# A grouped attention-pooling and per-sample product kernel: first group on raw fp32 operands, two-pass scores, work moved from VectorE to ScalarE and GpSimd

## The chip, the core and the metric

The kernel runs on one core of a Trainium2 chip. The core has TensorE for matrix products (PE in the trace; its weight loads are PEld), VectorE (DVE), ScalarE (ACT), GpSimd (POOL) and SyncE (SP), which issues most DMA. The engines share no clock and meet at semaphores. The metric is the device time of one execution in microseconds (us).

## What is computed

```
attn_in = tanh(einsum('bsd,da->bsa', hidden, W1) + b1)
scores = einsum('bsa,a->bs', attn_in, v)
masked_scores = where(mask, scores[:, None, :], NEG_INF)   # mask by type: prefix, postfix, all but self
p = softmax(masked_scores, axis=-1)
cnt = sum(mask, axis=-1)
pooled = einsum('bjl,bld->bjd', p, hidden) / cnt[..., None]
x = x + pooled
out = x + einsum('bsd,bdh->bsh', x, W[cat_ids]) + b[cat_ids][:, None, :]
```

x is 64 samples of 128 rows by 512 columns, W holds 64 matrices of 512x512, W1 is 512x128, all float32. With M = I + p/cnt (applied to rows) and Wi = W + I, the kernel computes for each sample k: z = x Wi, and out = z + (p/cnt) z + b, since both steps are linear in x.

## The kernel before

There are 16 groups (g) of G = 4 samples (k = 4g + b). x comes transposed, one 1 MB load per group (x_raw, two buffers); the matrix of each sample is one 1 MB load (w_raw, five buffers). Products are held to float32 quality by splitting each operand in a high part in the type fp32r (ScalarE copy, `w_hi`, `xT_hi`) and the rest (VectorE subtraction, `w_lo`, `xT_lo`), and adding three products: hi*hi, lo*hi, hi*lo. D = 512 is cut in DC = 4 chunks of 128, so x*Wi of one sample (`xw`, lines 498 to 511) is 12 matmuls of 128x512.

For each sample: VectorE adds the identity to the diagonal blocks of w_raw (`add_identity`, line 339, 128x512 elements); ScalarE makes w_hi (L255); VectorE makes w_lo (L363); TensorE does xw(k) into PSUM bank ps_y; ScalarE copies it to z_hi (L283), VectorE makes z_lo (L391); TensorE adds p z and the bias in four matmuls (`pz`, L519 to L522); ScalarE copies the sum to out_sb (L289) and SP stores it.

For each group: TensorE does x W1 (`hidden`, L474, 12 matmuls), ScalarE tanh (L261), TensorE the scores (`scores_group`: one matmul of v broadcast with attn, both plain float32, L482, and four small bf16 matmuls that add the mask, L484), VectorE the row maximum (L368), ScalarE four exp with row sums (L268), VectorE 1/(sum*count) and the scaling of the rows (L373, L376, L380), TensorE four transposes (L495), ScalarE and VectorE split the result (mix_hi L276, mix_lo L386).

Each engine's order is written by hand as a loop over k. An engine runs its list in order; a wait holds all that stands behind it. On TensorE a step is xw(k), pz(k-2), and then, by b: the transposes of group g (b = 0), hidden(g+1) (b = 1), scores(g+1) (b = 2), nothing (b = 3). VectorE makes w_lo two samples ahead, ScalarE w_hi three ahead. SP's list: store(k-3), the next x, and the matrix of sample k+7, which waits until w_lo(k+2) has freed its buffer. At the start 40 matmuls on zeros (`warm_up`) run while the first loads are under way; x of group 0 and W of sample 0 come in halves and are split half by half.

Of the kernel before, what the change touches and what calls it, by code (L numbers as in the profile page):

```python
# [25 lines left out]
def program(nc, xg, types, cats, w1, b1, v, w, bias, out):  # L27
# [9 lines left out]
    NX, NW, NH, NL, NZ, NO, NY = 2, 5, 4, 3, 3, 4, 5  # L37

    ctx = ExitStack()
    with ctx:  # L40
# [113 lines left out]
        @block.sync
        def _(sp):
            def load_w(k):
                cat = sp.value_load(cat_row[0:1, k:k + 1], min_val=0, max_val=C - 1)
# [24 lines left out]
            sp.dma_start(v_col[:], v.rearrange("(p a) -> p a", a=1)).then_inc(v_in, 16)  # L182
            sp.dma_start(b1_col[:], b1.rearrange("(p a) -> p a", a=1)).then_inc(b1_in, 16)
# [2 lines left out]
            load_w(2)
# [3 lines left out]
            for t in range(-2, B + 3):  # L190
# [48 lines left out]

# [351 lines left out]
```

## Time and profile before

| | |
|---|---|
| median of 3 runs | 335.98 us (335.58 to 336.35) |
| profiled execution | 336.02 us, span from first to last instruction 334.2 us |
| mean granted TensorE clock | 0.98 |
| PE busy | 317.1 us, 95% |
| DVE busy | 293.0 us, 88% |
| ACT busy | 257.0 us, 77% |
| POOL busy | 4.7 us, 1% |
| DMA | 101.56 MB, mean 304 GB/s |

The profiled execution lies on the median; 1.8 us of it are outside the span. Busy shares are averages over the start and the steady part of the kernel, which have different limits, and must be read stage by stage. Matmul records of TensorE overlap (one lasts 0.39 us, the next starts 0.23 us after it), so the time that one costs is read from the distance of starts.

### The profile page before, as it was taken

The page shows a single profiled execution, that of the slowest core. Times are in us where ns is not written, and L with a number is a line of the kernel's source. Part 1 is how long each engine was busy: PE and PEld are TensorE (multiplying, and loading weights), DVE is VectorE, ACT ScalarE, POOL GpSimd, SP SyncE. Part 2 cuts the span into 40 slices and gives each one's busy share as a digit, 9 for nine tenths or more (in the row PEclk, how much of TensorE's full clock was granted, in tenths as well). Part 3 has the DMA queues.
Part 4 walks back from the last instruction along what each step waited for, and adds up shares of the span by engine and source line. Part 5 has one row for each costly group of instructions (what it writes and reads, how often), then busy time and mean ns, then how long its engine had stood idle before and what let it go on. Part 6 is the DMA issues. An engine that isn't in the chain of part 4 may idle for free.

```text
span 334.2 us, 4766 instructions
## 1 busy us (share of the span) xinstructions
PE 317.1 (95%) x1416; PEld 251.7 (75%) x1416; DVE 293.0 (88%) x305; ACT 257.0 (77%) x373; POOL 4.7 (1%) x19
## 2 busy tenths in 40 slices
PE   7475899999999999999999999999999999999996
PEld 5253678787887878787887878787887878788784
DVE  1559969898998989898998989899998989899860
ACT  2468378796978879696978879697887879697843
POOL 5000000000000000000000000000000000000000
PEclk9969699999999999999999999999999999999999
DMA  6999777998989799898989899898979899784113
GB/s 151 349 424 421 271 297 267 363 328 251 402 289 420 234 373 345 281 381 259 416 267 387 299 370 349 305 351 272 393 261 394 296 335 375 279 273 176 63 63 126
DMA packets 21642, 101.56 MB, mean 304 GB/s; under 512 B 2706, under 2 KB 2706, under 8 KB 11634
## 3 DMA queue, kind: packets, MB, share of 16 engines
q1 hardware_dynamic: 21458, 100.94, 82.5%
q0 software_dynamic: 160, 0.33, 1.0%
q8 instruction: 12, 0.20, 0.2%
q14 instruction: 12, 0.10, 0.1%
HBM read 84.48 MB, written 16.78 MB: 303 GB/s over the span
## 4 chain that ended last, share of the span: by engine, by line
PE 89%; DMA 4%; DVE 3%; SPq 2%; issue 1%; ACT 0%; DVEq 0%
PE ps_y L507 17%; PE ps_y L509 17%; PE ps_y L508 17%; PE ps_pre L474 13%; PE ps_y L522 4%; PE ps_y L520 4%; PE ps_y L519 4%; PE ps_y L521 4%; DMA w_raw<-in_L_cond_W 4%; PE ps_scores L482 4%; PE ps_pT L495 2%; DVE w_lo L363 1%; PE ps_scores L484 1%; DVE xT_lo L350 1%; DVE w_raw L339 1%
## 5 line engine op out<-in xcount | busy, mean ns | idle before, releaser
L363 DVE TENSOR_TENSOR w_lo<-w_raw,w_hi 128x2048 fp32r<-128x2048 f32 x63 | 143.9, 2285 | 0.0
L255 ACT ACTIVATE w_hi<-w_raw 128x2048 fp32r<-128x2048 f32 x63 | 121.9, 1935 | 4.2 <-DVE w_raw L339 4.2
L507 PE MATMUL ps_y<-w_hi,xT_hi 128*128 128x512 f32 x256 | 104.2, 407 | 5.2 <-DVE w_lo L356 5.2
L509 PE MATMUL ps_y<-w_hi,xT_lo 128*128 128x512 f32 x256 | 101.2, 395 | 0.0
L508 PE MATMUL ps_y<-w_lo,xT_hi 128*128 128x512 f32 x256 | 100.6, 393 | 0.0
L507 PEld LDWEIGHTS ps_y<-w_hi,xT_hi 128*128 128x128 f32 x256 | 48.6, 190 | 14.7 <-DVE w_lo L356 5.6
L509 PEld LDWEIGHTS ps_y<-w_hi,xT_lo 128*128 128x128 f32 x256 | 48.6, 190 | 11.2
L508 PEld LDWEIGHTS ps_y<-w_lo,xT_hi 128*128 128x128 f32 x256 | 48.8, 191 | 9.7
L391 DVE TENSOR_TENSOR z_lo<-ps_y,z_hi 128x512 fp32r<-128x512 f32 x64 | 43.7, 684 | 6.0 <-ACT z_hi L283 6.0
L283 ACT ACTIVATE z_hi<-ps_y 128x512 fp32r<-128x512 f32 x64 | 39.4, 616 | 9.4 <-PE ps_y L509 9.4
L339 DVE TENSOR_TENSOR w_raw<-w_raw,ident 128x512 f32<-128x512 f32 x63 | 43.0, 683 | 3.4 <-DMA w_raw<-in_L_cond_W 3.4
L289 ACT ACTIVATE out_sb<-ps_y 128x512 f32<-128x512 f32 x64 | 40.1, 627 | 6.3 <-PE ps_y L522 6.3
L268 ACT ACTIVATE probs<-ps_scores,neg_max 128x128 f32<-128x128 f32 x64 | 22.7, 367 | 18.2 <-DVE neg_max L368 18.2
L350 DVE TENSOR_TENSOR xT_lo<-x_raw,xT_hi 128x2048 fp32r<-128x2048 f32 x15 | 34.3, 2286 | 0.0
L261 ACT ACTIVATE attn<-ps_pre,b_col 128x512 f32<-128x512 f32 x16 | 11.0, 688 | 25.2 <-PE ps_pre L474 25.2
L474 PE MATMUL ps_pre<-xT_hi,w_hi 128*128 128x512 f32 x64 | 26.4, 413 | 4.2 <-ACT w_hi L293 2.0
L244 ACT ACTIVATE xT_hi<-x_raw 128x2048 fp32r<-128x2048 f32 x15 | 29.1, 1940 | 0.0
L474 PE MATMUL ps_pre<-xT_hi,w_lo 128*128 128x512 f32 x64 | 26.0, 406 | 0.0
L474 PE MATMUL ps_pre<-xT_lo,w_hi 128*128 128x512 f32 x64 | 25.9, 404 | 0.0
L522 PE MATMUL ps_y<-b_both,one_hot 128*128 128x512 f32 x64 | 25.3, 395 | 0.0
L520 PE MATMUL ps_y<-z_hi,mix_lo 128*128 128x512 f32 x64 | 24.9, 389 | 0.0
L519 PE MATMUL ps_y<-z_hi,mix_hi 128*128 128x512 f32 x64 | 24.9, 389 | 0.0
(64 smaller groups left out, 257.7 us busy)
## 6 DMA issues: line engine op xcount, KB each, us to landing
w_raw<-in_L_cond_W SPq DMA_DIRECT2D x63, 1024.0 KB, 7.9
out<-out_sb SPq DMA_DIRECT2D x64, 256.0 KB, 6.6
x_raw<-in_x SPq DMA_DIRECT2D x15, 1024.0 KB, 10.5
x_raw<-in_x SPq DMA_DIRECT2D x2, 512.0 KB, 6.1
w_raw<-in_L_cond_W SPq DMA_DIRECT2D x2, 512.0 KB, 10.0
w_raw<-in_L_cond_W SPq DMA_DIRECT2D x1, 256.0 KB, 7.1
b_raw<-in_L_cond_b POOLq DMA_DIRECT2D x2, 128.0 KB, 8.5
type_all<-in_itok_B POOLq DMA_DIRECT2D x1, 32.0 KB, 6.9
```

Of the source, the lines that this page charges most:

```text
L255: nc.scalar.activation(w_hi[k % NH][:], w_raw[k % NW][:], ACT.Copy).then_inc(w_hi_ready, 1)
L283: nc.scalar.activation(z_hi[k % NZ][:], ps_y[k % NY][:], ACT.Copy).then_inc(z_hi_ready, 1)
L289: nc.scalar.activation(out_sb[k % NO][:], ps_y[k % NY][:], ACT.Copy).then_inc(out_ready, 1)
L339: nc.vector.tensor_tensor(diagonal(k % NW), diagonal(k % NW), eye.to_broadcast([P, DC, P]), ALU.add)\
L363: nc.vector.tensor_tensor(w_lo[k % NL][:], w_raw[k % NW][:], w_hi[k % NH][:].bitcast(F32), ALU.subtract).then_inc(w_lo_ready, 1)
L391: nc.vector.tensor_tensor(z_lo[k % NZ][:], ps_y[k % NY][:], z_hi[k % NZ][:].bitcast(F32), ALU.subtract).then_inc(z_lo_ready, 1)
L474: last = nc.tensor.matmul(ps_pre[:], wp[:, c, :], xp[g % NX][:, c, :], start=(c == 0 and i == 0), stop=(c == DC - 1 and i == 2))
L507: nc.tensor.matmul(y[:], xT_hi[q][:, c, xs], w_hi[k % NH][:, c, :], start=(c == 0), stop=False)
L508: nc.tensor.matmul(y[:], xT_hi[q][:, c, xs], w_lo[k % NL][:, c, :], start=False, stop=False)
L509: last = nc.tensor.matmul(y[:], xT_lo[q][:, c, xs], w_hi[k % NH][:, c, :], start=False, stop=(c == DC - 1))
L519: nc.tensor.matmul(y[:], mh, z_hi[k % NZ][:], start=False, stop=False, skip_group_check=True)
L522: nc.tensor.matmul(y[:], one_hot[:, k:k + 1].to_broadcast([P, P]), b_both[:], start=False, stop=True, skip_group_check=True).then_inc(pz_d ...
```

## The change

- **First group on raw operands.** For samples 0 to 3 x*Wi is done as four plain float32 matmuls on x_raw and w_raw (`xw_raw`), and x W1 of groups 0 and 1 as four plain float32 matmuls (`hidden_raw`). x of group 0 and W of samples 0 to 3 are not split. W1 is split later.
- **Third x buffer.** x_raw has three buffers (NX = 3); the split parts keep two (NT = 2).
- **Scores in two passes.** v is multiplied into attn by ScalarE (av_hi, fp32r) and VectorE (av_lo), and the scores are two fp32r matmuls with a matrix of ones, in place of one float32 matmul.
- **Rows scaled on ScalarE.** Four ScalarE copies of 128x128 with a per-row scale replace one VectorE multiplication of 128x512.
- **Identity on GpSimd.** `add_identity` is GpSimd's for all samples.
- **Orders and queues.** The first group is written out by hand on each engine; exp comes ahead of copy_out in its step; W1, b1 and v are loaded from ScalarE's queue; the type and bias loads of GpSimd's queue stand behind its identity additions of samples 0 to 2; 26 warm-up matmuls instead of 40; a load of x waits on an older x.

```diff
-    NX, NW, NH, NL, NZ, NO, NY = 2, 5, 4, 3, 3, 4, 5
+    NX, NT, NW, NH, NL, NZ, NO, NY = 3, 2, 5, 4, 3, 3, 4, 5
+    RAW = G
...
             def load_x(g):
-                if g >= NX:
-                    sp.wait_ge(xT_lo_ready, x_count(g - NX))
+                if g == NX:
+                    sp.wait_ge(xw_done, RAW)
+                elif g > NX:
+                    sp.wait_ge(xT_lo_ready, g - NX)
+                    sp.wait_ge(pre_done, g - NX + 1)
...
+            def add_identity(k):
+                pool.wait_ge(w_in[k % NW], 16 * (k // NW + (1 if k % NW else 0)))
+                nc.gpsimd.tensor_tensor(diagonal(k % NW), diagonal(k % NW), eye.to_broadcast([P, DC, P]), ALU.add)\
+                    .then_inc(wi_ready, 1)
...
                 nc.scalar.activation(attn[:], ps_pre[:], ACT.Tanh, bias=b1_col[:]).then_inc(attn_ready, 1)
+                act.wait_ge(attn_ready, g + 1)
+                nc.scalar.activation(av_hi[:], attn[:], ACT.Copy, scale=v_col[:]).then_inc(av_hi_ready, 1)
...
+            def scale_group(g):
+                act.wait_ge(scale_ready, g + 1)
+                for i in range(G):
+                    last = nc.scalar.activation(probs[:, i, :], probs[:, i, :], ACT.Copy, scale=row_scale[:, i:i + 1])
+                last.then_inc(probs_ready, 1)
...
+            def split_av_lo(g):
+                dve.wait_ge(av_hi_ready, g + 1)
+                nc.vector.scalar_tensor_tensor(av_lo[:], attn[:], v_col[:], av_hi[:].bitcast(F32),
+                                               ALU.mult, ALU.subtract).then_inc(av_lo_ready, 1)
...
-                nc.tensor.matmul(ps_scores[:], v_col[:].to_broadcast([P, P]), attn[:], start=True, stop=False)
+                nc.tensor.matmul(ps_scores[:], ones[:], av_hi[:], start=True, stop=False)
+                pe.wait_ge(av_lo_ready, g + 1)
+                nc.tensor.matmul(ps_scores[:], ones[:], av_lo[:], start=False, stop=False)
...
+            def xw_raw(k):
+                for c in range(DC):
+                    if k == 0 and c % HALF == 0:
+                        pe.wait_ge(wi_ready, c // HALF + 1)
+                    elif k >= 1 and c == 0:
+                        pe.wait_ge(wi_ready, wi_count(k))
+                    last = nc.tensor.matmul(ps_y[k][:], x_raw[0][:, c, k * S:(k + 1) * S], w_raw[k][:, c, :],
+                                            start=(c == 0), stop=(c == DC - 1))
+                last.then_inc(xw_done, 1)
...
-            warm_up(40)
-            pe.wait_ge(w1_hi_ready, 1)
-            hidden(0)
+            warm_up(26)
+            hidden_raw(0)
+            pe.wait_ge(consts_ready, 8)
+            xw_raw(0)
```

TensorE at the start of the kernel before: the warm-up, and the first matmuls of hidden(0) (ps_pre is its PSUM bank) with what they wait for.

```order
L527 MATMUL ps_y<-warm 128x256 x39
L474 MATMUL ps_pre<-xT_hi,w_hi 128x512 [waits xT_lo_ready,w1_hi_ready]
L474 MATMUL ps_pre<-xT_lo,w_hi 128x512
L474 MATMUL ps_pre<-xT_hi,w_lo 128x512 [waits w1_lo_ready]
L474 MATMUL ps_pre<-xT_hi,w_hi 128x512
```

TensorE at the same place after the change: the whole of hidden_raw(0), xw_raw(0) and the scores of group 0.

```order
L566 MATMUL ps_y<-warm 128x256 x25
L491 MATMUL ps_pre<-x_raw,w_raw 128x512 [waits x_in0,w1_in]
L491 MATMUL ps_pre<-x_raw,w_raw 128x512 x3
L534 MATMUL ps_y<-w_raw,x_raw 128x512 [waits wi_ready,consts_ready]
L534 MATMUL ps_y<-w_raw,x_raw 128x512
L534 MATMUL ps_y<-w_raw,x_raw 128x512 [waits wi_ready]
L534 MATMUL ps_y<-w_raw,x_raw 128x512
L510 MATMUL ps_scores<-av_hi,ones 128x512 [waits av_hi_ready]
L512 MATMUL ps_scores<-av_lo,ones 128x512 [waits av_lo_ready]
```

The waits on the split parts became waits on the loads and on GpSimd's additions, and the scores of group 0 now stand behind four matmuls of sample 0, not twelve.

ScalarE in the steady part of the kernel before, from the exp of one group to the x split of the next.

```order
L268 ACTIVATE probs,row_sum<-ps_scores,neg_max 128x128 [waits probsT_done,neg_max_ready]
L268 ACTIVATE probs,row_sum<-ps_scores,neg_max 128x128 x3
L255 ACTIVATE w_hi<-w_raw 128x2048 [waits xw_done,wi_ready]
L283 ACTIVATE z_hi<-ps_y 128x512 [waits pz_done,xw_done]
L289 ACTIVATE out_sb<-ps_y 128x512 [waits out_stored1,pz_done]
L244 ACTIVATE xT_hi<-x_raw 128x2048 [waits xw_done,x_in1]
```

ScalarE at the same place after the change.

```order
L299 ACTIVATE probs,row_sum<-ps_scores,neg_max 128x128 [waits probsT_done,neg_max_ready]
L299 ACTIVATE probs,row_sum<-ps_scores,neg_max 128x128 x3
L326 ACTIVATE out_sb<-ps_y 128x512 [waits out_stored0,pz_done]
L284 ACTIVATE w_hi<-w_raw 128x2048 [waits xw_done,wi_ready]
L320 ACTIVATE z_hi<-ps_y 128x512 [waits pz_done,xw_done]
L306 ACTIVATE probs<-probs,row_scale 128x128 [waits scale_ready]
L306 ACTIVATE probs<-probs,row_scale 128x128 x3
L326 ACTIVATE out_sb<-ps_y 128x512 [waits out_stored1,pz_done]
L278 ACTIVATE xT_hi<-x_raw 128x2048 [waits xw_done,x_in0]
```

Between exp and the split of x one more copy_out and four scalings now stand.

VectorE in the steady part after the change, from the split of x on (xT_lo) to the next maximum; the identity additions (L339) that stood behind each z_lo are gone, and av_lo is new.

```order
L376 TENSOR_TENSOR xT_lo<-x_raw,xT_hi 128x2048 [waits xT_hi_ready]
L383 TENSOR_TENSOR w_lo<-w_raw,w_hi 128x2048 [waits xw_done,w_hi_ready]
L405 TENSOR_TENSOR mix_lo<-ps_pT,mix_hi 128x512 [waits mix_hi_ready]
L410 TENSOR_TENSOR z_lo<-ps_y,z_hi 128x512 [waits z_hi_ready]
L383 TENSOR_TENSOR w_lo<-w_raw,w_hi 128x2048 [waits xw_done,w_hi_ready]
L388 SCALAR_TENSOR_TENSOR av_lo<-attn,v_col,av_hi 128x512 [waits av_hi_ready]
L410 TENSOR_TENSOR z_lo<-ps_y,z_hi 128x512 [waits z_hi_ready]
L393 TENSOR_REDUCE neg_max<-ps_scores 128x4 [waits scores_done]
```

The same stretch of VectorE before.

```order
L350 TENSOR_TENSOR xT_lo<-x_raw,xT_hi 128x2048 [waits xT_hi_ready]
L363 TENSOR_TENSOR w_lo<-w_raw,w_hi 128x2048 [waits xw_done,w_hi_ready]
L386 TENSOR_TENSOR mix_lo<-ps_pT,mix_hi 128x512 [waits mix_hi_ready]
L391 TENSOR_TENSOR z_lo<-ps_y,z_hi 128x512 [waits z_hi_ready]
L339 TENSOR_TENSOR w_raw<-w_raw,ident 128x4x128 [waits w_in4]
L363 TENSOR_TENSOR w_lo<-w_raw,w_hi 128x2048 [waits xw_done,w_hi_ready]
L391 TENSOR_TENSOR z_lo<-ps_y,z_hi 128x512 [waits z_hi_ready]
L339 TENSOR_TENSOR w_raw<-w_raw,ident 128x4x128 [waits w_in0]
L368 TENSOR_REDUCE neg_max<-ps_scores 128x4 [waits scores_done]
```

Two additions fell out of this stretch and one av_lo came in.

## Rows read from the trace of the kernel before

**Rows 1.** The page: busy time by engine, and the chain that ended last.

```profile
PE 317.1 (95%) x1416; PEld 251.7 (75%) x1416; DVE 293.0 (88%) x305; ACT 257.0 (77%) x373; POOL 4.7 (1%) x19
...
PE 89%; DMA 4%; DVE 3%; SPq 2%; issue 1%; ACT 0%; DVEq 0%
```

**Rows 2.** Busy time by stretch: engines, granted clock, DMA share, GB/s.

```profile
19.00:25.00 6.00, 5.81 (x13) 4.48 (x14) 2.69 (x2) 4.35 (x4) 0.00 (x0) 0.50 1.01 419
...
170.00:189.00 19.00, 19.00 (x88) 15.23 (x87) 18.01 (x19) 15.79 (x24) 0.00 (x0) 1.00 0.93 336
```

**Rows 3.** Timeline, where hidden(2) starts on TensorE.

```profile
55.79 0.39 PE L474 MATMUL ps_pre<-xT_hi,w_hi 128*128 128x512 f32 x1
```

**Rows 4.** Timeline of the start: warm-up, first matmuls, and what loads ended.

```profile
1.07 6.36 PE L527 MATMUL ps_y<-warm 128*128 128x256 bf16 x40 [1.07 <-DVE warm L394]
...
9.41 0.50 PE L474 MATMUL ps_pre<-xT_hi,w_hi 128*128 128x512 f32 x1 [1.98 <-ACT w_hi L293]
...
9.97 1.06 ACT L238 ACTIVATE xT_hi<-x_raw 128x1024 fp32r<-128x1024 f32 x1 [0.61 <-DMA x_raw<-in_x]
...
12.86 0.43 DVE L335 TENSOR_TENSOR w_raw<-w_raw,ident 128x256 f32<-128x256 f32 x1 [0.58 <-DMA w_raw<-in_L_cond_W]
...
19.19 0.79 PE L507 MATMUL ps_y<-w_hi,xT_hi 128*128 128x512 f32 x1 [5.21 <-DVE w_lo L356]
...
22.32 0.69 DVE L339 TENSOR_TENSOR w_raw<-w_raw,ident 128x512 f32<-128x512 f32 x1 [3.39 <-DMA w_raw<-in_L_cond_W]
```

**Rows 5.** Timeline of TensorE, one steady group: start us, duration, engine, line.

```profile
169.78 0.39 PE L474 MATMUL ps_pre<-xT_hi,w_hi 128*128 128x512 f32 x1
...
176.20 1.02 PE L482 MATMUL ps_scores<-attn,v_col 128*128 128x512 f32 x2
177.06 0.39 PE L484 MATMUL ps_scores<-penalty,ident_bf 128*128 x4
177.25 0.47 PE L507 MATMUL ps_y<-w_hi,xT_hi 128*128 128x512 f32 x1
```

**Rows 6.** Timeline of ScalarE, one steady group; idle before in brackets.

```profile
159.18 0.37 ACT L268 ACTIVATE probs<-ps_scores,neg_max 128x128 f32<-128x128 f32 x1 [1.21 <-DVE neg_max L368]
...
160.56 1.93 ACT L255 ACTIVATE w_hi<-w_raw 128x2048 fp32r<-128x2048 f32 x1
162.37 0.60 ACT L283 ACTIVATE z_hi<-ps_y 128x512 fp32r<-128x512 f32 x1
162.85 0.61 ACT L289 ACTIVATE out_sb<-ps_y 128x512 f32<-128x512 f32 x1
163.32 1.94 ACT L244 ACTIVATE xT_hi<-x_raw 128x2048 fp32r<-128x2048 f32 x1
...
172.76 0.69 ACT L261 ACTIVATE attn<-ps_pre,b_col 128x512 f32<-128x512 f32 x1 [1.46 <-PE ps_pre L474]
```

**Rows 7.** Timeline of VectorE, one steady group.

```profile
158.45 0.69 DVE L368 TENSOR_REDUCE neg_max<-ps_scores 128x4 f32<-128x512 f32 x1 [0.88 <-PE ps_scores L484]
159.06 2.28 DVE L363 TENSOR_TENSOR w_lo<-w_raw,w_hi 128x2048 fp32r<-128x2048 f32 x1
161.26 0.68 DVE L391 TENSOR_TENSOR z_lo<-ps_y,z_hi 128x512 fp32r<-128x512 f32 x1
...
166.87 2.29 DVE L350 TENSOR_TENSOR xT_lo<-x_raw,xT_hi 128x2048 fp32r<-128x2048 f32 x1
```

**Rows 8.** Groups of instructions: the identity additions on VectorE, and GpSimd's work.

```profile
L339 DVE TENSOR_TENSOR w_raw<-w_raw,ident 128x512 f32<-128x512 f32 x63 | 43.0, 683 | 3.4 <-DMA w_raw<-in_L_cond_W 3.4
...
L207 POOL MEMSET penalty<- 128x384 bf16 x1 | 0.4, 437 | 0.0
L209 POOL TENSOR_SCALAR_AFFINE_SELECT ident<-ident 128x128 f32<-128x128 f32 x1 | 0.3, 295 | 0.2 <-POOL penalty L207 0.2
```

**Rows 9.** DMA issues of the page: the bias load, KB each, us to landing.

```profile
b_raw<-in_L_cond_b POOLq DMA_DIRECT2D x2, 128.0 KB, 8.5
```

More of the change, by code:

```diff
@@ L50, in program @@
         x_raw = [sb(f"x_raw{i}", [P, DC, GS], F32) for i in range(NX)]
-        xT_hi = [sb(f"xT_hi{i}", [P, DC, GS], F32R) for i in range(NX)]
-        xT_lo = [sb(f"xT_lo{i}", [P, DC, GS], F32R) for i in range(NX)]
+        xT_hi = [sb(f"xT_hi{i}", [P, DC, GS], F32R) for i in range(NT)]
+        xT_lo = [sb(f"xT_lo{i}", [P, DC, GS], F32R) for i in range(NT)]
         w_raw = [sb(f"w_raw{i}", [P, DC, D], F32) for i in range(NW)]
@@ L59, in program @@
         attn = sb("attn", [P, GS], F32)
+        av_hi = sb("av_hi", [P, GS], F32R)
+        av_lo = sb("av_lo", [P, GS], F32R)
         probs = sb("probs", [P, G, S], F32)
@@ L181, in _ @@
                     .then_inc(w0_in[h], 16)
[L182 to L183 removed]
             load_w(1)
+            load_w(2)
             load_x(1)
[L186 removed]
             load_w(3)
             load_w(4)
[L190 removed]
+            load_w(5)
+            load_x(2)
+            load_w(6)
+            for t in range(B + 3):
                 g, b = t // G, t % G
@@ L353, in split_w0_lo, with split_xT_lo @@
-            def split_w0_lo(h):
-                c = slice(h * HALF, (h + 1) * HALF)
-                dve.wait_ge(w_hi_ready, h + 1)
-                nc.vector.tensor_tensor(w_lo[0][:, c, :], w_raw[0][:, c, :], w_hi[0][:, c, :].bitcast(F32),
-                                        ALU.subtract).then_inc(w_lo_ready, 1)
+            def split_xT_lo(g):
+                dve.wait_ge(xT_hi_ready, g)
+                nc.vector.tensor_tensor(xT_lo[g % NT][:], x_raw[g % NX][:], xT_hi[g % NT][:].bitcast(F32),
+                                        ALU.subtract).then_inc(xT_lo_ready, 1)
@@ L529, in _ @@
             pe.wait_ge(warm_ready, 1)
-            warm_up(40)
-            pe.wait_ge(w1_hi_ready, 1)
-            hidden(0)
+            warm_up(26)
+            hidden_raw(0)
+            pe.wait_ge(consts_ready, 8)
+            xw_raw(0)
             pe.wait_ge(kinds_ready, 1)
-            pe.wait_ge(consts_ready, 8)
+            pe.wait_ge(ones_ready, 1)
             kinds = [load_kind(i) for i in range(G)]
-            for k in range(B + 2):
+            scores_group(0, kinds)
+            xw_raw(1)
+            kinds = [load_kind(G), load_kind(G + 1)]
+            xw_raw(2)
+            kinds += [load_kind(G + 2), load_kind(G + 3)]
+            transpose_probs(0)
+            hidden_raw(1)
+            xw_raw(3)
+            scores_group(1, kinds)
+            pe.wait_ge(bias_ready, 2)
+            pz(0)
+            pz(1)
+            for k in range(G, B + 2):
                 g, b = k // G, k % G
```

275 lines of the change are left out of this document (137 added, 138 removed).

## Prediction

> **What bounds the kernel now.** I read the page first: TensorE is busy 95% of the span and holds 89% of the chain that ended last [rows 1]. Shares are averages, so I then read the busy times by stretch. In a steady stretch of 19 us, the period of one group, TensorE is busy 19.00 us at clock 1.00, VectorE 18.01, ScalarE 15.79, GpSimd nothing, and the DMA engines are 93% busy at 336 GB/s [rows 2]. So from hidden(2) on, which starts at 55.79 us [rows 3], the time is TensorE's matmuls laid end to end; VectorE comes second with 1 us of slack in a group. Ahead of that the kernel is bound otherwise: the first product starts at 9.41, the first xw only at 19.19 after 5.21 us of waiting for w_lo, at clock 0.50 [rows 2, 4]. TensorE waits there for splits that wait for loads. Hence two questions: what one steady group costs after the change, and when hidden(2) starts.
>
> **The steady group on TensorE.** The float32 matmul of the scores is two instructions; from 176.20 to the mask matmuls at 177.06 it costs 0.86 us [rows 5]. An fp32r matmul costs 0.23 us: hidden and xw with the four of pz between 169.78 and 176.20 are 28 matmuls in 6.42 us [rows 5]. Two of them make 0.46, so a group gets 0.40 us shorter: 18.6 us. After hidden(2) starts, 14 scores remain (groups 2 to 15): 14 x 0.40 = 5.6 us. Bounds: 0 if the mask matmuls, whose addresses come from registers, were ready no earlier than now; 5.6 otherwise. I take 5.6, as 0.86 us of matmul is replaced outright.
>
> **Does another engine stop this?** ScalarE: from start to start a w_hi takes 1.81, z_hi 0.48, copy_out 0.47, four exps 1.38 (159.18 to 160.56) [rows 6]. Added are av_hi, 0.47 to 0.69 (the nearest rows are the copy and the tanh), with a wait for its own tanh; and four scalings, between 0.47 (one copy of as many elements) and 1.38 (the exps, which also sum). I take 0.6 and 1.0: 15.8 + 1.6 = 17.4 of 18.6 us. In order of time, with 0 at the xw behind the scores: exp at 1.0 as now (159.18 against 158.2), to 2.3; copy_out 2.8; w_hi 4.6; z_hi 5.1; scalings 6.1, where the transposes come only after two xw and two pz, 7.4; copy_out 6.6; xT_hi 8.4; then VectorE's xT_lo 8.5 to 10.7. Hidden starts at 169.78 - 158.2 = 11.6 [rows 5], so xT_lo has 0.9 us to spare; now it ends at 169.1 with 0.6 to spare [rows 5, 7]. tanh follows hidden's end (0.2 late as now), av_hi ends at 15.8, and the scores want it at 18.0. Exp now stands ahead of copy_out, so ScalarE arrives earlier and waits longer there, which costs nothing.
>
> VectorE: a w_lo or xT_lo takes 2.20 from start to start, a small operation 0.60 [rows 7]. It loses four identity additions (0.68 each as recorded [rows 8], 0.60 as spaced) and the scaling of rows, 3.0 us in all, and gains av_lo, 0.60: 18.0 - 3.0 + 0.6 = 15.6 of 18.6 us. av_lo stands behind w_lo in its step: 16.3 to 16.9, wanted at 18.2. What queues behind its wait is z_lo, wanted a step later.
>
> GpSimd: the operation is not in the trace. Nearest are the select of 128x128 float32 in 0.295 us (one input) and the memset of 128x384 in 0.437 [rows 8]. By elements the select gives 1.2 us for 128x512; a second input may double it, 2.4; the memset bounds it at 0.4 from below. I take 1.2. A matrix is loaded seven samples ahead and its addition needed three ahead, so a few us more on that path are hidden; GpSimd is busy 5 of 18.6 us, at most 10.
>
> What does GpSimd do to VectorE beside it? No row has both at work on data of this size, so it is bounded from nothing to the full addition: 0 to 1.2 us of VectorE for each sample, 15.6 to 20.4 us a group. If half of each addition falls beside z_lo, mix_lo, the maximum or idle time, the exposed part is about 0.6: 15.6 + 2.4 = 18.0, still under 18.6, though the spares of 0.9 and 1.3 us are then used now and then. I put 0.1 us a group for that, 1.4 us in all, with bounds 0 and 25 (14 x 1.8).
>
> The page "SBUF — State Buffer" of the Trainium skill, section "Who interferes with whom", speaks against this change: a VectorE instruction with two SBUF inputs and a GpSimd instruction that reads SBUF exclude each other, the second waits for the first to finish. By it the four w_lo, the xT_lo and av_lo of a group would queue with the four additions, while z_lo, mix_lo and the maximum, which read PSUM, would not. "GPSIMD Engine Reference", section 3.1, states 4497 ns for a two-input addition of 2048 elements a partition; a quarter is an estimate of 1.1 us, near the value from the rows. The rival below has this as a mechanism of this kernel.
>
> DMA: loads and stores of a group in 18.6 instead of 19.0 us bring 93% to 95%. The third x buffer starts a load of x earlier, not more loads. Hidden.
>
> **The start.** The last of x(0) and W1 to be used lands at about 9.9 [rows 4]; the same 1.3 MB now come from two queues: hidden_raw(0) starts at 9.8. (The bounds: 8.5 and 10.5.) The 40 warm-up matmuls end at 7.4 us, 0.16 us each; 26 end about 2.2 us earlier, so TensorE has idled some 4.5 us by then. After 2.0 us of idling the clock was 1.00, after 5.2 it was 0.50 for 6 us [rows 2, 4]. I take the low clock for hidden_raw(0): four products of 0.86 are 3.4 us at full clock, 6.6 with 6 us of half: 16.4. The first half of W(0) lands at 12.9 [rows 4], and the additions of both halves are done ahead of 16.4. From here, at 3.4 us for each xw_raw or hidden_raw: xw_raw(0) 19.8, scores(0) 20.5, xw_raw(1) 23.9, xw_raw(2) 27.4, transposes 27.7, hidden_raw(1) 31.2, xw_raw(3) 34.6, scores(1) 35.3, two pz 37.1, xw(4) 39.9, pz 40.8. Loads: the DMA engines run at 419 GB/s there, 1 MB in 2.5 us, and x(1) with W(2) were landed at 22.3 [rows 2, 4]; each comes ahead of its use (W(2) at 20, x(1) 22.5, W(3) 25, W(4) 27.5).
>
> TensorE is then overtaken by ScalarE's list: tanh(1) and av_hi from 31.3 to 32.5, w_hi(4) 34.3, z_hi 34.8, w_hi(5) 36.6, z_hi 37.1, exp (after the maximum at 37.9) 39.4, copy_out 39.8, w_hi(6) 41.6, scalings 42.6. The transposes of group 1 wait for these from 40.8 to 42.7. Then copy_out 43.1, xT_hi(2) 44.9, VectorE's xT_lo(2) 47.2. TensorE has xw(5) and pz done at 46.8, so **hidden(2) starts at 47.2**, 8.6 us earlier than now. Ahead of tanh(1) ScalarE also waits for the bias load, which GpSimd issues after its third addition, at about 21; with 8.5 us to landing [rows 9] that is 29.5, just in time. Bounds of the start: 44.2 if the clock stays high (3 us earlier), 50 if the bias or the additions are late.
>
> **The sum.** 47.2 + (334.2 - 55.79) - 5.6 + 1.4 = 321.2 us of span. With 1.8 outside it (336.02 - 334.2), 323.0. The profiled execution lies on the median of 335.98, so no shift.
>
> **Rivals.** (A) GpSimd's additions hold up VectorE in full, where each finds VectorE between two large subtractions: it becomes the bound at 15.6 + 4 x 1.2 = 20.4 us a group; 321.6 + 14 x 1.8 = 346.8, slower. It decides from 1.0 us exposed for each sample: (19.6 - 15.6)/4, as 14.4/14 = 1.0 us a group eats the gain. For it: VectorE has large two-input work for 11.6 of its 15.6 us. Against it: behind three of the four w_lo stands a z_lo or mix_lo, and some idle time. 12%. (B) The same in part, 0.75 to 0.95 exposed, or xT_lo too late for hidden by up to 0.8 us a group: 327 to 333, middle 329. 17%. (C) The start is better than worked out, clock at full from 9.8 on: hidden(2) at 44.2 and no contention, 318.6. 11%. (D) The forecast, 320 to 327: 60%.
>
> **How the numbers follow.** The likeliest is D, 323.0. The range takes in D, nearly all of B and C: 317.5 to 334; A and the ends are left out. Faster by over 0.2% (0.7 us, about what a measurement of this kernel can tell from no change): D, C, B, 0.87. Slower: A, 0.12. Within: 0.01.
>
> **What would show it.** Right: the period of a group in the stretches is 18.6 with TensorE busy throughout, av_hi and av_lo matmuls spaced 0.23, hidden(2) at 44 to 50, VectorE about 16 to 18 busy in 18.6. The clock at 10 to 16 us shows the low-clock step; ScalarE without waits between 31 and 45 shows that it is the bound there. Wrong: mean durations of w_lo above 2.3 us (contention), TensorE waiting at hidden for xT_lo, at the scores for av_lo, or at pz(0) for the bias; a GpSimd addition of over 2 us.

## The result, and the profile after

The changed kernel takes 327.9 us (median of 4 runs, 327.67 to 328.25) against 335.88 for the kernel before, a ratio of 0.9762 with a 95% interval of 0.9745 to 0.9779. Forecast were 323.0 us and a range of 317.5 to 334.0. The time is inside the range, in the part that the prediction gave to rival B (327 to 333) and not in that of the forecast (320 to 327); the gain is 8.0 us where 13.0 were worked out, and it is made up otherwise than forecast. The profiled execution took 328.25 us, its span is 326.4 us, and its mean granted clock is 1.00.

The page of the changed kernel: busy time, the chain that ended last, and, from its groups (line, engine, operation, count, busy us, mean ns, idle before), GpSimd's additions and two groups of VectorE.

```profile
PE 313.0 (96%) x1378; PEld 241.9 (74%) x1378; DVE 277.8 (85%) x233; ACT 274.1 (84%) x446; POOL 127.2 (39%) x85
...
PE 35%; DVE 22%; ACT 21%; issue 14%; DMA 6%; SPq 1%; POOL 1%; ACTq 0%
...
L231 POOL TENSOR_TENSOR w_raw<-w_raw,ident 128x512 f32<-128x512 f32 x63 | 120.5, 1913 | 165.1 <-DMA w_raw<-in_L_cond_W 165.1
L383 DVE TENSOR_TENSOR w_lo<-w_raw,w_hi 128x2048 fp32r<-128x2048 f32 x60 | 148.2, 2469 | 6.9 <-ACT w_hi L284 6.9
...
L388 DVE SCALAR_TENSOR_TENSOR av_lo<-attn,v_col,av_hi 128x512 fp32r<-128x512 f32 x16 | 25.8, 1612 | 6.3 <-ACT av_hi L292 6.3
```

Against [rows 1], TensorE is still the busiest engine, but its share of the chain fell from 89% to 35%: VectorE, ScalarE and "issue" (time in which an engine waited for nothing that the profile shows) came in. That is the first sign of a new wait in the steady part. A w_lo now takes 2469 ns in the mean (2285 before), and av_lo, an operation of the size of z_lo, takes 1612.

TensorE's timeline of the changed kernel: hidden_raw(0), the transposes of group 1, hidden(2); then hidden of two later groups and of two groups in the middle.

```profile
6.54 3.67 PE L491 MATMUL ps_pre<-x_raw,w_raw 128*128 128x512 f32 x8
...
38.52 0.66 PE L525 MATMUL ps_pT<-ident,probs 128*128 128x128 f32 x4 [2.25 <-ACT probs L306]
...
43.31 0.47 PE L502 MATMUL ps_pre<-xT_hi,w_hi 128*128 128x512 f32 x1 [0.49 <-issue]
...
64.28 0.39 PE L502 MATMUL ps_pre<-xT_hi,w_hi 128*128 128x512 f32 x1
...
82.88 0.39 PE L502 MATMUL ps_pre<-xT_hi,w_hi 128*128 128x512 f32 x1
...
159.74 0.39 PE L502 MATMUL ps_pre<-xT_hi,w_hi 128*128 128x512 f32 x1
...
179.08 0.39 PE L502 MATMUL ps_pre<-xT_hi,w_hi 128*128 128x512 f32 x1
```

These starts split the result in two. hidden(2) starts at 43.3 us instead of 55.8 [rows 3]: the start gave 12.5 us. What follows takes 326.4 - 43.3 = 283.1 us, before 334.2 - 55.8 = 278.4: the steady part lost 4.7 us. Its first period is the longest, 20.97 us (43.31 to 64.28). It is 18.60 once (64.28 to 82.88) and between 18.87 and 19.65 in the others, 19.34 in the middle (159.74 to 179.08); before it was 19.0 throughout.

The first period: VectorE's two w_lo and its av_lo ahead of the scores of group 2, and the second scores matmul, which waited for av_lo.

```profile
43.14 3.37 DVE L383 TENSOR_TENSOR w_lo<-w_raw,w_hi 128x2048 fp32r<-128x2048 f32 x1
...
47.63 2.82 DVE L383 TENSOR_TENSOR w_lo<-w_raw,w_hi 128x2048 fp32r<-128x2048 f32 x1
50.38 1.75 DVE L388 SCALAR_TENSOR_TENSOR av_lo<-attn,v_col,av_hi 128x512 fp32r<-128x512 f32 x1
```

```profile
52.17 0.50 PE L512 MATMUL ps_scores<-av_lo,ones 128*128 128x512 f32 x1 [1.97 <-DVE av_lo L388]
```

Three instructions are longer here than undisturbed (2.28 us for a w_lo, 0.74 for av_lo), by 2.6 us together, and TensorE stood idle for 1.97.

Where the extra time of a group in the middle lies, in three timelines of the same stretch: TensorE at the scores, VectorE, GpSimd.

```profile
166.16 0.40 PE L510 MATMUL ps_scores<-av_hi,ones 128*128 128x512 f32 x1
166.97 0.50 PE L512 MATMUL ps_scores<-av_lo,ones 128*128 128x512 f32 x1 [0.42 <-DVE av_lo L388]
```

```profile
162.45 2.77 DVE L383 TENSOR_TENSOR w_lo<-w_raw,w_hi 128x2048 fp32r<-128x2048 f32 x1
165.14 1.78 DVE L388 SCALAR_TENSOR_TENSOR av_lo<-attn,v_col,av_hi 128x512 fp32r<-128x512 f32 x1
...
168.36 2.28 DVE L383 TENSOR_TENSOR w_lo<-w_raw,w_hi 128x2048 fp32r<-128x2048 f32 x1
```

```profile
161.77 1.30 POOL L231 TENSOR_TENSOR w_raw<-w_raw,ident 128x512 f32<-128x512 f32 x1 [5.42 <-DMA w_raw<-in_L_cond_W]
164.92 1.45 POOL L231 TENSOR_TENSOR w_raw<-w_raw,ident 128x512 f32<-128x512 f32 x1 [1.85 <-DMA w_raw<-in_L_cond_W]
169.10 2.70 POOL L231 TENSOR_TENSOR w_raw<-w_raw,ident 128x512 f32<-128x512 f32 x1 [2.73 <-DMA w_raw<-in_L_cond_W]
```

An addition undisturbed takes 1.26 to 1.3 us. The one at 164.92 began 0.2 us ahead of av_lo's start, when w_lo was still under way, and lasted 0.2 longer. av_lo lasted 1.78 us, against 0.74 in the two groups where no addition was under way. The w_lo ahead of it is long as well, 2.77 us against 2.28: the addition at 161.77 had begun before it. av_lo's end, 166.92, is what the second scores matmul waited for. The start of this matmul lies 0.81 us behind the first, where 0.23 is the distance of matmuls that don't wait. The addition at 169.10 began inside the w_lo of 168.36 and lasted 2.70 us: some 1.5 us that were left of w_lo, and its own 1.26. So an addition and a VectorE instruction with two SBUF inputs take turns, and each lasts longer by the other's rest.

### The profile page after: what moved, and what is told of

Read it like the earlier page. It is cut to its first block, busy times and chain, and to the rows that moved or that the text cites. A ratio compares the mean times of both kernels' runs of the same rounds, so it can differ in the third digit from the quotient of the medians.

```text
span 326.4 us, 4763 instructions
## 1 busy us (share of the span) xinstructions
PE 313.0 (96%) x1378; PEld 241.9 (74%) x1378; DVE 277.8 (85%) x233; ACT 274.1 (84%) x446; POOL 127.2 (39%) x85
## 4 chain that ended last, share of the span: by engine, by line
PE 35%; DVE 22%; ACT 21%; issue 14%; DMA 6%; SPq 1%; POOL 1%; ACTq 0%
DVE w_lo L383 11%; PE ps_y L546 7%; PE ps_y L548 7%; PE ps_y L547 7%; ACT xT_hi L278 5%; ACT w_hi L284 5%; DVE av_lo L388 5%; ACT probs L299 4%; PE ps_pre L502 3%; ACT probs L306 3%; DMA w_raw<-in_L_cond_W 3%; ACT out_sb L326 3%; DMA b_raw<-in_L_cond_b 3%; DVE mix_lo L405 2%; PE ps_scores L512 2%
## 5 line engine op out<-in xcount | busy, mean ns | idle before, releaser
L231 POOL TENSOR_TENSOR w_raw<-w_raw,ident 128x512 f32<-128x512 f32 x63 | 120.5, 1913 | 165.1 <-DMA w_raw<-in_L_cond_W 165.1
L383 DVE TENSOR_TENSOR w_lo<-w_raw,w_hi 128x2048 fp32r<-128x2048 f32 x60 | 148.2, 2469 | 6.9 <-ACT w_hi L284 6.9
L284 ACT ACTIVATE w_hi<-w_raw 128x2048 fp32r<-128x2048 f32 x60 | 116.2, 1937 | 0.0
L546 PE MATMUL ps_y<-w_hi,xT_hi 128*128 128x512 f32 x240 | 96.5, 402 | 0.0
L548 PE MATMUL ps_y<-w_hi,xT_lo 128*128 128x512 f32 x240 | 93.9, 391 | 0.0
L547 PE MATMUL ps_y<-w_lo,xT_hi 128*128 128x512 f32 x240 | 93.5, 389 | 0.0
L546 PEld LDWEIGHTS ps_y<-w_hi,xT_hi 128*128 128x128 f32 x240 | 45.1, 188 | 8.8 <-DVE w_lo L383 0.3
L299 ACT ACTIVATE probs<-ps_scores,neg_max 128x128 f32<-128x128 f32 x64 | 22.7, 367 | 23.9 <-DVE neg_max L393 23.9
L388 DVE SCALAR_TENSOR_TENSOR av_lo<-attn,v_col,av_hi 128x512 fp32r<-128x512 f32 x16 | 25.8, 1612 | 6.3 <-ACT av_hi L292 6.3
L560 PE MATMUL ps_y<-z_lo,mix_hi 128*128 128x512 f32 x64 | 24.9, 389 | 0.0
L502 PE MATMUL ps_pre<-xT_hi,w_hi 128*128 128x512 f32 x56 | 22.2, 396 | 0.5 <-issue 0.5
L502 PE MATMUL ps_pre<-xT_hi,w_lo 128*128 128x512 f32 x56 | 22.1, 394 | 0.0
```

What stands on the lines that cost most here:

```text
L231: nc.gpsimd.tensor_tensor(diagonal(k % NW), diagonal(k % NW), eye.to_broadcast([P, DC, P]), ALU.add)\
L284: nc.scalar.activation(w_hi[k % NH][:], w_raw[k % NW][:], ACT.Copy).then_inc(w_hi_ready, 1)
L383: nc.vector.tensor_tensor(w_lo[k % NL][:], w_raw[k % NW][:], w_hi[k % NH][:].bitcast(F32), ALU.subtract).then_inc(w_lo_ready, 1)
L388: nc.vector.scalar_tensor_tensor(av_lo[:], attn[:], v_col[:], av_hi[:].bitcast(F32), ALU.mult, ALU.subtract).then_inc(av_lo_ready, 1)
L502: last = nc.tensor.matmul(ps_pre[:], wp[:, c, :], xp[g % NT][:, c, :], start=(c == 0 and i == 0), stop=(c == DC - 1 and i == 2))
L546: nc.tensor.matmul(y[:], xT_hi[q][:, c, xs], w_hi[k % NH][:, c, :], start=(c == 0), stop=False)
```

## Experiments

All times are beside the kernel before (335.75 to 336.1 us) on the same chip as the run.

**1. No identity from sample 8 on.**

```diff
-            for k in range(3, B):
+            for k in range(3, 8):
                 add_identity(k)
...
-                act.wait_ge(wi_ready, wi_count(k))
+                if k >= 8:
+                    act.wait_ge(w_in[k % NW], 16 * (k // NW + (1 if k % NW else 0)))
+                else:
+                    act.wait_ge(wi_ready, wi_count(k))
```

> Left out: the identity is not added for samples 8 to 63, so their x term is missing from the output; GpSimd is idle from there on and w_hi waits for the load alone. Theory (GpSimd's addition shuts VectorE out, and av_lo, 1.78 us long where an addition runs and 0.74 where not, is what TensorE waits for): av_lo is 0.74 us in all groups, w_lo 2.29, the gap of up to 0.9 us ahead of the second scores matmul goes, the period of a group falls from 19.3 to 18.6 us, and 14 groups give 9 to 10 us: 318. Rival (av_lo is late because it stands behind w_lo on VectorE and behind tanh and av_hi on ScalarE, whatever GpSimd does): period stays at 19.0 or more, 324 to 328.

Measured: 319.6 us, span 318.1, ratio 0.950 (0.947 to 0.952). The groups of VectorE, av_lo of one group with the weight load of its matmul, and hidden of two groups in a row on TensorE:

```profile
L386 DVE TENSOR_TENSOR w_lo<-w_raw,w_hi 128x2048 fp32r<-128x2048 f32 x60 | 137.1, 2285 | 14.8 <-ACT w_hi L287 14.8
...
L391 DVE SCALAR_TENSOR_TENSOR av_lo<-attn,v_col,av_hi 128x512 fp32r<-128x512 f32 x16 | 11.9, 745 | 5.8 <-ACT av_hi L295 5.8
```

```profile
161.81 0.75 DVE L391 SCALAR_TENSOR_TENSOR av_lo<-attn,v_col,av_hi 128x512 fp32r<-128x512 f32 x1
```

```profile
163.25 0.19 PEld L515 LDWEIGHTS ps_scores<-av_lo,ones 128*128 128x128 f32 x1
```

```profile
156.83 0.39 PE L505 MATMUL ps_pre<-xT_hi,w_hi 128*128 128x512 f32 x1
...
175.42 0.39 PE L505 MATMUL ps_pre<-xT_hi,w_hi 128*128 128x512 f32 x1
```

Without GpSimd's additions all 16 av_lo take some 0.74 us, and the period is 18.6, the number that was worked out for TensorE alone. av_lo, undisturbed, is done at 162.56, 0.7 us ahead of the load of its matmul's weights at 163.25: that is its spare. From hidden(2), at 45.0 here, to the end it is 273.1 us, 10.0 less than in the changed kernel. That is the price of the additions from sample 8 on; 2.2 us of it lie in the first period (20.97 against 18.74 here). The rival (av_lo late by its place in the order) is out. This kernel does less work, so it shows the price but not that it can be saved.

**2. Scores in one float32 pass.**

```diff
-                nc.tensor.matmul(ps_scores[:], ones[:], av_hi[:], start=True, stop=False)
-                pe.wait_ge(av_lo_ready, g + 1)
-                nc.tensor.matmul(ps_scores[:], ones[:], av_lo[:], start=False, stop=False)
+                nc.tensor.matmul(ps_scores[:], v_col[:].to_broadcast([P, P]), attn[:], start=True, stop=False)
...
-                nc.scalar.activation(av_hi[:], attn[:], ACT.Copy, scale=v_col[:]).then_inc(av_hi_ready, 1)
```

> The changed kernel with the scores as before, one float32 matmul of v with attn, without av_hi and av_lo; the rest of the change stays. Theory (the wait for av_lo costs more than the 0.40 us that two passes save): nothing waits for av_lo, the period is 19.0 us in every group as in the kernel before, 14 x 0.3 us better than the changed kernel: 323 to 324, and 2 us more gone at the scores of group 2. Rival (two passes pay in spite of the wait, and the longer period comes from elsewhere, w_lo held up by GpSimd): 14 x 0.4 worse, 332 to 334.

Measured: 325.3 us, ratio 0.9685 (0.9665 to 0.9706); span 323.2. Two groups in a row:

```profile
158.68 0.39 PE L495 MATMUL ps_pre<-xT_hi,w_hi 128*128 128x512 f32 x1
...
177.67 0.39 PE L495 MATMUL ps_pre<-xT_hi,w_hi 128*128 128x512 f32 x1
```

The period is 18.99, as before the change, although the additions still run on GpSimd and w_lo still takes 2381 ns in the mean. So at a period of 19.0 the additions hurt only through av_lo, and every other spare of the schedule holds; at 18.6 that was not tried. From hidden(2) to the end it is 323.2 - 44.6 = 278.6 us, 4.5 less than in the changed kernel: so much the two passes cost there, instead of saving 5.6. In the whole time 2.6 us are left of it (3.2 by the profiled spans), as hidden(2) started 1.3 later, at 44.6, and that is also what the time lies above the expected 323 to 324. The later start isn't the edit's own: an addition caught VectorE's row_div of group 1 (1/(sum*count), four elements to a partition; 1.26 us long, 0.15 in the changed kernel), TensorE waited 2.5 us for the scalings, and its granted clock then fell to 0.50 (39 to 40 us).

**3. Additions back on VectorE from sample 8 on.**

```diff
-            for k in range(3, B):
+            for k in range(3, 8):
                 add_identity(k)
...
                 split_z_lo(k - 1)
+                if k + 4 < B:
+                    add_identity_vector(k + 4)
```

> The changed kernel with the additions of samples 8 to 63 back on VectorE, behind z_lo as in the kernel before; GpSimd idle from there. VectorE then has 15.6 + 4 x 0.60 = 18.0 us of work in a group of 18.6. Theory (contention, not the amount of work, is the loss): av_lo 0.74 us, period 18.6 to 18.8, 318 to 321. Rival (VectorE is the bound either way, so that the additions had to leave it): period 19.0 or more, 325 to 330.

Measured: 320.45 us, ratio 0.955 (0.952 to 0.959). Two groups in a row:

```profile
155.71 0.39 PE L514 MATMUL ps_pre<-xT_hi,w_hi 128*128 128x512 f32 x1
...
174.40 0.39 PE L514 MATMUL ps_pre<-xT_hi,w_hi 128*128 128x512 f32 x1
```

With one instruction stream in place of two that shut each other out the kernel is 7 us faster. The period is 18.76 in the mean of the groups: 0.16 above TensorE's own 18.6, with VectorE at some 18.0 of work. So the move to GpSimd wasn't needed for the gain: as it was made, it cost 7 us. What a move to GpSimd can give at best is the 0.16 us a group, some 2 us; experiment 4 has 1.8.

**4. The same additions on GpSimd at another moment.**

```diff
             for k in range(3, B):
+                if k >= 8:
+                    g, b = (k - 4) // G, k % G
+                    if b == 2 and g + 1 < GROUPS:
+                        pool.wait_ge(av_lo_ready, g + 2)
+                    else:
+                        pool.wait_ge(w_lo_ready, w_count(k - 2))
                 add_identity(k)
```

> The changed kernel, but GpSimd waits with each addition from sample 8 on until VectorE begins work that reads PSUM: behind w_lo of the sample two ahead, and in the step with av_lo behind av_lo. Same work, same engines, another moment. Theory (an exclusive port, so that the moment decides): av_lo 0.74 us, additions 1.26 us, period 18.6 to 18.8, 318 to 320. Rival (any addition beside VectorE slows it by its whole length wherever it falls): VectorE 15.6 + 5.0 = 20.6 us a group, 340 or more. Rival (the additions come too late for w_hi when they wait): ScalarE waits for GpSimd, 328 or more.

Measured: 318.7 us, ratio 0.9486 (0.9466 to 0.9505), and 318.6 us, ratio 0.9496 (0.9476 to 0.9516), on another occasion. It is the fastest kernel of the study. Two groups in a row on TensorE, then VectorE and GpSimd at the place shown above for the changed kernel:

```profile
154.85 0.39 PE L508 MATMUL ps_pre<-xT_hi,w_hi 128*128 128x512 f32 x1
...
173.44 0.39 PE L508 MATMUL ps_pre<-xT_hi,w_hi 128*128 128x512 f32 x1
```

```profile
157.63 2.41 DVE L389 TENSOR_TENSOR w_lo<-w_raw,w_hi 128x2048 fp32r<-128x2048 f32 x1
159.97 0.74 DVE L394 SCALAR_TENSOR_TENSOR av_lo<-attn,v_col,av_hi 128x512 fp32r<-128x512 f32 x1
160.63 0.67 DVE L416 TENSOR_TENSOR z_lo<-ps_y,z_hi 128x512 fp32r<-128x512 f32 x1
162.16 0.69 DVE L399 TENSOR_REDUCE neg_max<-ps_scores 128x4 f32<-128x512 f32 x1 [0.86 <-PE ps_scores L520]
```

```profile
156.59 1.30 POOL L231 TENSOR_TENSOR w_raw<-w_raw,ident 128x512 f32<-128x512 f32 x1 [4.83 <-DVE w_lo L389]
160.78 1.29 POOL L231 TENSOR_TENSOR w_raw<-w_raw,ident 128x512 f32<-128x512 f32 x1 [2.89 <-DVE av_lo L394]
```

The same instructions on the same engines, 9.2 us faster. The addition at 156.59 lies beside mix_lo and z_lo, which read PSUM, and lengthens w_lo by 0.13 us; the one at 160.78 lies beside z_lo and idle time and lengthens nothing. z_lo is 0.67 us with an addition beside it, as without. So an addition isn't a cost in itself: it costs what is left of it when VectorE's next instruction with two SBUF inputs begins. The period is 18.6, as without any additions, 1.8 us in all less than with the additions on VectorE (experiment 3), and from hidden(2) on it takes 273.1 us, the same as in experiment 1.

**5. and 6. What brought the first product forward.** In the changed kernel hidden_raw(0) starts at 6.5 us, 3.3 us ahead of the forecast. Two parts of the queues were undone, one in each kernel: the load of the types, which in the changed kernel stands behind the identity additions of sample 0, and W1 in ScalarE's queue.

```diff
+            pool.dma_start(type_all[:], types.rearrange("(a n) -> a n", a=1).to_broadcast([P, B]))\
+                .then_inc(types_in, 16)
             pool.dma_start(type_in[:], types.rearrange("(a n) -> a n", a=1)).then_inc(type_row_in, 16)
```

> The changed kernel with the load of the types to all partitions (32 KB, an entry to each partition) again first on GpSimd's queue, at 1.3 us. hidden_raw(0) started at 6.5 us, not at the 9.8 forecast. Theory (this small load stood in the first data's way in the kernel before): hidden_raw(0) starts at 8 to 9 us. Rival (it was W1 in ScalarE's own queue): still 6.5 us.

```diff
             load_x(0)
+            sp.dma_start(w1_raw[:], w1).then_inc(w1_in, 16)
...
-            act.dma_start(w1_raw[:], w1).then_inc(w1_in, 16)
```

> The changed kernel with W1 loaded from SP's queue behind x of group 0, in place of ScalarE's. Theory of the types load: W1 lands soon after x, hidden_raw(0) at 6.5 to 7.2 us. Rival (a queue of its own brings W1 early): 8 us or later.

Measured, one execution each: 329.1 and 326.4 us. The first product, with the types load first, and with W1 behind x:

```profile
7.57 3.67 PE L491 MATMUL ps_pre<-x_raw,w_raw 128*128 128x512 f32 x8 [2.10 <-DMA x_raw<-in_x]
```

```profile
7.83 3.70 PE L491 MATMUL ps_pre<-x_raw,w_raw 128*128 128x512 f32 x8 [2.34 <-DMA w_raw<-in_L_cond_W]
```

Against the changed kernel's profile the types load costs 1.0 us of x's landing (7.6, just under the expected 8 to 9), and W1 behind x costs 1.3. But the profiles of the other kernels that load in the changed kernel's way have their first product between 6.4 and 7.0 us, so by one execution each these are some 0.6 to 1.1 and 0.8 to 1.4 us. Both theories were half right, and the two parts together are about 2 of the 3.3 us; the rest was not sought. hidden(2) started at 44.1 and 43.4, against 43.3. From there to the end it is 283.2 and 281.2 us, against 283.1: the first kernel's end is later by its start, and the second's is earlier by its steady part, where the second scores matmuls came late by 6.2 us in sum (8.1 in the changed kernel) with the same work. By one execution I don't ascribe that.

**7. Eight warm-up matmuls instead of 26.**

```diff
-            warm_up(26)
+            warm_up(8)
```

> The changed kernel with 8 warm-up matmuls instead of 26, so that TensorE idles for some 3 to 4 us ahead of hidden_raw(0). It tests the step of the prediction that took the low clock there. If an idle TensorE of this length loses its clock: granted clock 0.5 for a stretch between 6 and 14 us, hidden_raw(0) 6.5 us long and not 3.6, and about 3 us later at scores(0); the end moves by 0 to 3 us, since later steps wait for ScalarE. If not: clock 1.00 throughout and 326 to 328 us.

Measured, one execution: 327.4 us. The first product, then the weight loads of its matmuls on the profile's PEld:

```profile
6.64 5.54 PE L491 MATMUL ps_pre<-x_raw,w_raw 128*128 128x512 f32 x8 [3.69 <-DMA x_raw<-in_x]
```

```profile
8.48 0.34 PEld L491 LDWEIGHTS ps_pre<-x_raw,w_raw 128*128 128x128 f32 x1 [0.52 <-issue]
9.34 0.34 PEld L491 LDWEIGHTS ps_pre<-x_raw,w_raw 128*128 128x128 f32 x1 [0.52 <-issue]
...
10.73 0.19 PEld L491 LDWEIGHTS ps_pre<-x_raw,w_raw 128*128 128x128 f32 x1 [0.24 <-issue]
```

After 3.7 us of idling the loads come 0.86 us apart up to about 10.2 us, then 0.43: TensorE worked at half pace, that of the lower of its two levels (1.2 GHz), for 3.6 us where the prediction took 6, and the product took 5.5 instead of 3.7. So the mechanism of that step of the prediction exists. It was not met in the changed kernel, where the warm-up ran right into the first product, nor in experiments 5 and 6, where TensorE idled 2.1 and 2.3 us ahead of a product of 3.7. Whether the 1.9 us lost here reach the rest isn't told by this execution: hidden(2) started at 45.1, 1.8 later than in the changed kernel, but an addition had caught row_div of group 1 here (1.25 us long), and hidden(2) started just as late, at 45.0, in experiment 1, which lost nothing at its first product.

**8. The kernel before with the new queues alone.**

```diff
-            sp.dma_start(w1_raw[:], w1).then_inc(w1_in, 16)
...
+            pool.dma_start(type_all[:], types.rearrange("(a n) -> a n", a=1).to_broadcast([P, B]))\
+                .then_inc(types_in, 16)
...
+            act.dma_start(w1_raw[:], w1).then_inc(w1_in, 16)
```

The types load moves behind GpSimd's constants, and b1 and v move to ScalarE's queue with W1.

> The kernel before with the queues alone changed: W1, b1 and v from ScalarE's queue, the types load behind GpSimd's constants. It asks how much of the start's gain (hidden(2) 12.5 us earlier) is the queues' and how much is the raw products'. Theory (raw products, since the splits are what TensorE waits for from 14 to 19 and 29 to 35 us): hidden(0) at 7, hidden(2) at 54 to 55.8, 334 to 336 us. Rival (earlier landing carries through): hidden(2) at 52 or earlier, 332 or less.

Measured: 336.3 us, ratio 1.0002 (0.999 to 1.0014). The first product of hidden(0) and of hidden(2):

```profile
8.03 0.47 PE L474 MATMUL ps_pre<-xT_hi,w_hi 128*128 128x512 f32 x1
...
56.28 0.39 PE L474 MATMUL ps_pre<-xT_hi,w_hi 128*128 128x512 f32 x1
```

The first product comes 1.4 us earlier and hidden(2) not at all. So the 12.5 us of the start are not the queues'. What is left of the change for them are the raw products with the order written for them. That they alone do it was not tried.

A part of the 12.5 us is TensorE's clock. Before the change it works at a granted clock of 0.50 not only from 19 to 25 us [rows 2], after 5.21 us of waiting for w_lo, but again ahead of hidden(2), after 3.50 and 1.18 us of waiting (for the transposes of group 0 and for hidden(1)). The second stretch in the kernel before:

```profile
36.00:39.00 3.00, 3.00 (x8) 2.32 (x8) 3.00 (x4) 0.00 (x0) 0.00 (x0) 0.51 0.30 66
```

From hidden(1) to hidden(2) it is 21.03 us there, 2.0 more than a period of 19.0. In the changed kernel the granted clock is 1.00 all through the start, and the longest wait is 2.25 us. Half of the 6 us, and these 2.0, are 5 us: an estimate of the most that the clock gave back. The kernel of this experiment still had both stretches.

**9. Another order around sample 4, on top of experiment 4.**

```diff
                     copy_out(0)
+                    scale_group(1)
+                    split_xT_hi(2)
                     split_w_hi(6)
+                    copy_out(1)
+                    split_w_hi(7)
...
+            split_z_lo(3)
+            split_xT_lo(2)
+            split_w_lo(6)
```

> The kernel with gated additions, and another order at sample 4: ScalarE does the scalings of group 1 and xT_hi(2) ahead of w_hi(6), VectorE z_lo(3) and xT_lo(2) ahead of w_lo(6). TensorE waited 2.3 us for the scalings ahead of the transposes of group 1 and 0.6 us at hidden(2). Theory (ScalarE's order is the bound there): transposes at 37.2 and not 38.3, hidden(2) at 41.2 and not 43.1, the end 1 to 2 us earlier: 317. Rival (the work only moves, and w_lo(6) or the scores of group 2 wait instead): 318.5 to 320.

> The kernel with gated additions once more, on the same chip as the reordered one, for a ratio of the two: 318.7 by both theories.

Measured: 322.4 us, ratio 0.959 (0.957 to 0.962), slower than experiment 4 (318.6 beside it), against theory. Two matmuls of xw(5) and hidden(2) on TensorE, with its stretch from 40 to 45 us, on VectorE what the scalings waited for, then the w_hi of sample 8 on ScalarE:

```profile
40.34 0.63 PE L561 MATMUL ps_y<-w_hi,xT_hi 128*128 128x512 f32 x1
40.77 0.63 PE L562 MATMUL ps_y<-w_lo,xT_hi 128*128 128x512 f32 x1
...
44.70 0.39 PE L517 MATMUL ps_pre<-xT_hi,w_hi 128*128 128x512 f32 x1
```

```profile
40.00:45.00 5.00, 5.00 (x17) 3.93 (x16) 4.27 (x2) 5.00 (x5) 0.00 (x0) 0.67 0.99 412
```

```profile
33.13 3.08 DVE L394 TENSOR_TENSOR w_lo<-w_raw,w_hi 128x2048 fp32r<-128x2048 f32 x1
36.13 1.24 DVE L409 TENSOR_TENSOR row_div<-row_sum,seen 128x4 f32<-128x4 f32 x1
```

```profile
48.61 1.92 ACT L290 ACTIVATE w_hi<-w_raw 128x2048 fp32r<-128x2048 f32 x1 [2.38 <-POOL w_raw L231]
```

row_div, four elements to a partition and 0.16 us by itself, lasted 1.24 us, as the addition of sample 7, which isn't gated, was under way; w_lo ahead of it lasted 3.08. So the scalings, moved forward, began at 37.6 us, later by 1.1 for row_div and by up to 0.8 for w_lo, and ScalarE stood idle for 2.4 us in front of them. TensorE waited 2.76 us for them, and its granted clock then fell to the lower level: until 43.3 us the matmuls come 0.43 apart and not 0.23, so hidden(2), whose xT_lo was ready at 43.0, started at 44.7. Then the gate of sample 8 hung on w_lo(6), which the new order had put back, and w_hi(8) waited 2.4 us for GpSimd; av_hi and the scores of group 2 stand behind it, and the first period is 22.5 us (18.7 in experiment 4).

The profiled execution is the slowest of four, 323.37 us. The one with a mean granted clock of 1.00 took 321.4, still 2.8 above experiment 4: so much is not the clock's. A row_div caught is not the new order's doing, as experiments 1, 2 and 7 had it in the old one; its share was not measured apart. The bound of the start is thus not ScalarE's order alone; the additions on GpSimd and the clock hold it too.

## Why the prediction was right, point by point

- **TensorE bounds the steady part; two passes save 0.40 us a group.** Right in size where nothing waits: the period is 18.6 us (experiments 1 and 4), and 273.1 us from hidden(2) to the end, where the sum had 278.4 - 5.6 = 272.8.
- **ScalarE doesn't bind.** Right. The scalings took 1.2 us a group (1.0 assumed), and ScalarE still waited for the maximum, 23.9 us in the 16 groups.
- **GpSimd's addition.** 1.2 us by the nearest row, 1.26 measured alone, 1.9 in the mean with its waits.
- **What it does to VectorE: the step that failed.** The prediction counted that half of each addition would fall beside z_lo and the like, and put 0.1 us a group for it, 1.4 us in all. Measured are 10.0 us, 0.7 a group. The amount of work was judged well: 2.4 us a group were counted, and a w_lo is 0.18 us longer in the mean and av_lo 0.87 (against experiment 1), 1.6 us a group. What was wrong is the spare of av_lo, worked out as 1.3 us and used "now and then": it is 0.7 us (experiment 1), and it is used nearly each time. An addition that arrives during a w_lo, 2.2 us long, waits to its end and then goes first; the next instruction in that step is av_lo, which has two SBUF inputs and pays 1.04 of the addition's 1.26 us. 12 of the 14 av_lo of groups 2 to 15 lasted 1.75 to 1.79 us, those of groups 3 and 15 0.74.
- **Two more terms of the same wait.** In three groups (7, 10 and 11) av_lo alone is long, and their periods are 18.87 to 19.00. In eight groups the w_lo ahead of it is long too, 2.60 to 2.94 us, as an earlier addition was under way when it began, and the periods are 19.26 to 19.65. In group 2 two w_lo and av_lo are long, and the period is 20.97. In group 15 av_lo is short, yet its matmul waited, behind w_lo of 3.39 and 2.48 us. So av_lo is where the delay ends up; not all of it is made there.
- **Rival B** named a size that fits the period (up to 0.8 us a group) and the time (327 to 333), but the wrong waits (xT_lo, or the amount of work); it had 17%. The list of what would show the forecast wrong did name the scores waiting for av_lo, and a w_lo above 2.3 us (2.47 measured).
- **The Trainium skill's rule** ("SBUF — State Buffer", "Who interferes with whom"): the runs agree with it where they touch it. Two SBUF inputs against a GpSimd instruction that reads SBUF: av_lo's 0.74 becomes 1.78 us. PSUM and one SBUF input: z_lo 0.67 us with an addition beside it. The second waits for the first to finish: 1.26 plus the rest of w_lo.
- **Rival A** (VectorE held up in full, slower than before) is out: it needed 1.0 us exposed for each sample, and the 1.6 us a group are 0.4.
- **The start.** hidden(2) at 43.3, forecast 47.2, bounds 44.2 to 50: earlier than the lower bound. One profile tells it to within 2 us only: where the start is the same it came at 42.9 to 43.4 us in four profiles, and at 45.0 and 44.6 in experiments 1 and 2, where an addition had caught row_div. The chain of reasons held: TensorE runs through the first group almost without waits, then ScalarE's list holds the transposes of group 1 (2.25 us waited, 1.9 forecast) and xT_hi(2) with xT_lo(2) behind it comes last. Two terms were off: the first load lands at 6.5 and not 9.8, and the half pace was not met. Both put everything some 5 us early up to scores(1) (30.1 against 35.3), of which 3.9 were left at hidden(2).
- **The sum** came out 4.9 us too low in time. The start was 3.9 us better, the steady part 8.9 worse (283.1 against 278.4 - 5.6 + 1.4 = 274.2), of which 8.6 are contention beyond the 1.4 that were counted. The part outside the span was 1.8 us as counted (328.25 - 326.4), but the profiled execution lies 0.35 above the median, which takes 0.3 off. That makes 4.7; the other 0.2 is in the prediction's addition, whose terms give 321.4 us of span and not 321.2. Direction and range were right, and that the number came this near is luck in part: a start better than forecast hid almost half of what the contention cost.

## What to carry to other kernels

When work is moved to GpSimd while VectorE keeps large instructions with two SBUF inputs, don't count busy time but look which short instruction stands behind each large one, who waits for it, and how small its spare is: arrivals gather at the ends of the large ones, and a delay adds up along a row of such instructions. Start the GpSimd instruction by a wait on the VectorE instruction behind which the PSUM work stands; here that alone was worth 9 us. Leaving the additions on VectorE was worth 7. And test each part of a bundle apart: with the additions ungated, two-pass scores cost more than they save; with the additions gated or on VectorE, the period lies below the 19.0 of one-pass scores. Gated additions with one-pass scores were not run.
